# A four-layer perceiver on one core: late keys and values of layer four stored compactly, two units per context turn

## The reference, cut to what matters

```python
x = x + tanh(g_xattn[0]) * linear_attention(norm(x), ctx, mask)     # 16 heads
x = x + tanh(g_ffn[0])   * ternary_ffn(norm(x))
x = x + tanh(g_xattn[1]) * window_attention(norm(x), ctx)           # needs ctx rows 0..55 only
x = x + tanh(g_ffn[1])   * top2_of_16_experts(norm(x))
x = x + tanh(g_xattn[2]) * perceiver_attention(ctx, norm(x), mask)  # 8 heads, over ctx and latents
x = x + tanh(g_ffn[2])   * int8_ffn(norm(x))
x = x + tanh(g_xattn[3]) * attention(q=norm(x), k=ctx, v=ctx)       # 16 heads of 8
x = x + tanh(g_ffn[3])   * top2_of_8_experts(norm(x))
```

## Time and profile before

| | us |
|---|---|
| median of 3 runs | 881.52 (877.07 to 884.06) |
| the profiled execution | 890.45 |
| its span | 888.7 |
| PE, DVE, ACT, POOL busy | 758.9, 611.2, 415.3, 332.2 |

### The profile page before, as it was taken

The page is one execution under the profiler, slowest core; times in us unless marked ns, Lnnn a source line. Parts: engine busy times, 40 slices in busy tenths (PEclk is TensorE's granted clock), DMA queues, the critical chain, the costliest instruction groups (busy, mean ns, idle before and its releaser), DMA issues.

```text
span 888.7 us, 15989 instructions
## 1 busy us (share of the span) xinstructions
PE 758.9 (85%) x5636; PEld 500.2 (56%) x5636; DVE 611.2 (69%) x1270; ACT 415.3 (47%) x698; POOL 332.2 (37%) x269
## 2 busy tenths in 40 slices
PE   4699999974676678999699999998689999988996
PEld 4577777764444347664355555564336666554664
DVE  4789999994687425655656655557689999815652
ACT  2566666670454242452354454531027777654331
POOL 1765555550533440254087777750140000000111
PEclk9899999987888975999799999999959999999999
DMA  7366766423517533020504222207604565500220
GB/s 196 105 216 230 255 224 204 134 75 103 91 53 222 168 125 89 28 80 26 140 19 120 78 72 72 72 1 100 143 1 123 126 171 135 152 1 24 80 98 22
DMA packets 56610, 97.18 MB, mean 109 GB/s; under 512 B 16970, under 2 KB 41034, under 8 KB 55226
## 3 DMA queue, kind: packets, MB, share of 16 engines
q1 hardware_dynamic: 56546, 96.32, 38.0%
HBM read 64.65 MB, written 31.65 MB: 108 GB/s over the span
## 4 chain that ended last, share of the span: by engine, by line
PE 41%; DVE 32%; DMA 8%; ACT 6%; POOL 5%; issue 4%; SPq 3%; POOLq 0%; DVEq 0%; ACTq 0%
DVE arena L2324 8%; PE ps L1106 8%; DVE arena L1730 7%; PE ps L1096 6%; DMA d_v<-arena 5%; DVE rn L1885 4%; DVE arena L1934 3%; PE ps L1039 3%; PE ps L1274 2%; PE ps L1284 2%; PE ps L1209 2%; DVE arena L1913 2%; PE ps L1198 2%; DVE arena L1893 2%; ACT arena L1535 2%
## 5 line engine op out<-in xcount | busy, mean ns | idle before, releaser
L2324 DVE TENSOR_REDUCE arena<-ps 112x1 f32<-112x500 f32 x192 | 115.5, 669 | 15.1 <-PE ps L1183 14.2
L1730 DVE TENSOR_TENSOR arena<-ps,arena 128x448 f32<-128x448 f32 (+7 forms) x138 | 83.3, 628 | 60.5 <-ACT arena L1558 19.4
L1700 POOL TENSOR_TENSOR arena<-arena 125x448 f32<-125x448 f32 x96 | 109.6, 1142 | 24.1 <-ACT arena L1512 21.1
L1535 ACT ACTIVATE arena<-ps 125x896 f32<-125x896 f32 x96 | 87.0, 917 | 27.0 <-PE ps L1198 26.4
L1106 PE MATMUL ps<-arena 125*128 125x448 f32 (+1 forms) x208 | 97.0, 548 | 1.6 <-ACT arena L1512 1.2
L1592 POOL TENSOR_TENSOR arena<-arena 112x4 f32<-112x4 f32 x9 | 9.3, 1029 | 232.7 <-DVE arena L1754 226.7
L1512 ACT ACTIVATE arena<-arena,kbias 125x448 f32<-125x448 f32 x96 | 63.7, 668 | 65.3 <-DVE arena L1730 46.3
L1730 DVE TENSOR_TENSOR arena<-ps,rn 125x448 f32<-125x448 f32 x96 | 59.3, 618 | 47.7 <-PE ps L1096 43.3
L1096 PE MATMUL ps<-arena 128*125 128x448 f16 (+3 forms) x312 | 77.6, 359 | 3.0 <-DVEq L1741 3.0
L1096 PEld LDWEIGHTS ps<-arena 128*125 128x125 f16 (+1 forms) x312 | 40.8, 135 | 57.2 <-issue 42.3
L794 PE MATMUL ps<-w_k2h,arena 128*125 128x512 f16 x288 | 67.6, 387 | 6.1 <-ACT arena L1344 6.1
(11 more groups left out here) (308 smaller groups left out, 1477.3 us busy)
## 6 DMA issues: line engine op xcount, KB each, us to landing
d_k<-arena SPq DMA_DIRECT2D x24, 375.0 KB
d_v<-arena SPq DMA_DIRECT2D x24, 375.0 KB
arena<-d_k SPq DMA_DIRECT2D x96, 93.8 KB
arena<-d_v SPq DMA_DIRECT2D x8, 1008.0 KB
arena<-in_ctxT SPq DMA_DIRECT2D x8, 750.0 KB, 10.3
d_cln<-arena SPq DMA_DIRECT2D x8, 750.0 KB
d_clnT<-arena SPq DMA_DIRECT2D x8, 750.0 KB
arena<-d_clnT SPq DMA_DIRECT2D x8, 750.0 KB
```

Of the source, the lines that this page charges most:

```text
L1535: act.activation(p3[t % 2].rearrange("p (k h) q -> p k (h q)", k=2), ps[0:KP, 2 * (t % 2):2 * (t % 2) + 2, 0:8 * S], ACT.Exp).then_inc(l3_ ...
L1700: ins = pool.tensor_tensor(psum2[p][0:rows], psum2[p][0:rows], pexp[(t + p) % 2][0:rows], ALU.add)
L1730: return dve.tensor_tensor(out, a, b, op)
L2324: dve.tensor_reduce(mx3[bn % 2][:, u % 2, u % 8 // 2, u // 8:u // 8 + 1], ps[0:TT, max_bank_of(bn, u), 0:500], AX.X, ALU.max).then_inc(l3_ ...
```

## The change

- The f16 keys are stored as high and low alone (16 rows for 24 per four-head group), and the values as 128 columns instead of the padded 192. ACT copies the values in one piece; POOL's duplicate copy goes. Layer four loads the high part twice, and POOL spreads the values into the padded block (`spread_values3`) before PE uses it.
- Two units go with each turn (0 to 15), eight (16 to 23) with the chain, none inside layer two's attention; four buffers instead of three, and two f32 key buffers.
- The small loads of layer two go out after the turn of batch 6, and the 56 context rows per batch are loaded already turned (`c56T`), right after the pass; PE's transposes and ACT's copy of them go.
- In layer four, keys have three buffers in two parts; 8 maxima tiles instead of 4 run ahead of a batch (`MAX_AHEAD`), `turn_maxima` stands two steps before the last of a batch, the first scores of the next batch stand in the last step, and ACT writes both shift rows. DVE builds batch 0's query block from PSUM, ACT copies the queries for the others.
- At the last expert of both mixtures, DVE adds the earlier sum and the last term to `x` itself (`weigh_last`); POOL's loops over experts are written out.

```diff
-L1_LOADS = 5
+L1_LOADS = 4
+SETS = 4
...
-UNITS = [(b, 0) for b in range(B)] + [(b, third) for b in (7, 6, 0, 1, 2, 3, 4, 5) for third in (1, 2)]
-
-PRODUCT = {"latent_q": 14, "latent_k": 18, "latent_qT": 19, "queries2": 20}
...
+MAX_AHEAD = 32
 MAX_ORDER = [(0, u) for u in range(24)]
 for _b in range(1, B):
-    MAX_ORDER += [(_b, 0), (_b, 1), (_b - 1, TURN)] + [(_b, u) for u in range(2, 24)]
+    MAX_ORDER += [(_b, u) for u in range(4)] + [(_b - 1, TURN)] + [(_b, u) for u in range(4, 24)]
...
+            at = 500 * ((u - 18) % 3)
+            return wex[(u - 18) // 3][:, at:at + 500]
...
                 sp.wait_ge(d_free, 6 * b + 3 + 3)
                 sp.dma_start(batch(d_cln, b), cln[p].rearrange("p j d -> p (j d)")).then_inc(st[p], 16)
                 if more:
-                    sp.wait_ge(a_full, a_uses(b) + 8)
+                    sp.wait_ge(a_full, a_uses(b) + 10)
                     load_turned(b + 2, p)
                     sp.wait_ge(l0_rhs, b + 1)
                     load_context(b + 2, p)
+                if b == B - 1:
+                    store_later(2 * b)
+                    store_later(2 * b + 1)
+                    sp.wait_ge(ctx_done, 1)
+                    sp.dma_start(c56T, io["c56T"]).then_inc(l1_ld, 16)
                 sp.wait_ge(d_free, 6 * b + 3 + 6)
                 sp.dma_start(batch(d_clnT, b), clnT[p]).then_inc(st[p], 16)
-                store_later(b)
+                if b < B - 1:
+                    store_later(2 * b)
+                    store_later(2 * b + 1)
 
             def load_later(u):
                 b, third = UNITS[u]
...
+                if b == 6:
+                    for dst, name in ((w_l1, "L1_w"), (w_col1, "L1_cols"), (w_r1, "L1_router")):
+                        sp.dma_start(dst, io[name]).then_inc(l1_ld, 16)
...
-            store_later(8)
             sp.wait_ge(l0_att, 1)
...
-            for u in range(10, 13):
+            for u in range(16, 24):
                 store_later(u)
+                if u == 20:
+                    sp.wait_ge(lv_full, 20 - IN_TURNS + 1)
+                    load_experts1(0, 0)
+            sp.wait_ge(lv_full, 23 - IN_TURNS + 1)
+            load_experts1(1, 1)
             sp.wait_ge(rn_sq, 1)
-            for u in range(18, 24):
-                load_later(u)
-            for u in range(13, 24):
-                store_later(u)
-                if u == 14:
-                    sp.wait_ge(lv_full, 14 - B + 1)
-                    load_experts1(0, 0)
-                if u == 17:
-                    sp.wait_ge(lv_full, 17 - B + 1)
-                    load_experts1(1, 1)
-            sp.wait_ge(lv_full, 23 - B + 1)
             for dst, name in ((w_kT2, "L2_wkT"), (w_vT2, "L2_wvT"), (w_o2, "L2_wo"), (w_q2, "L2_wq"),
                               (qk_col, "qk_cols")):
                 sp.dma_start(dst, io[name]).then_inc(ld_m, 16)
@@ -628,8 +626,8 @@
 
             for p in range(2):
...
+                src = d_k3[b].rearrange("g e (d s) c -> e s d g c", s=2)
+                both = d_k3[b].rearrange("g e r c -> e r g c")
                 for hh in range(4):
-                    sp.dma_start(kst[p][32 * hh + 8:32 * hh + 32, :, at:at + 500], src[hh, :, :, at:at + 500])\
-                        .then_inc(l3_ld[p][u], 16)
+                    sp.dma_start(kst[p][32 * hh + 8:32 * hh + 24, :, cols], both[hh, :, :, cols]).then_inc(l3_ld[p][part], 16)
+                    sp.dma_start(kst[p][32 * hh + 24:32 * hh + 32, :, cols], src[hh, 0, :, :, cols])\
+                        .then_inc(l3_ld[p][part], 16)
...
+            for b in range(B - 2):
+                if b + 3 < B:
+                    sp.wait_ge(l3_s0, KT * b + 4)
+                    sp.wait_ge(l3_s, KT * b + 4)
+                    load_keys3(b + 3, b % 3, 0)
+                sp.wait_ge(l3_v, b + 1)
+                load_values3(b + 2, b % 2)
+                if b + 3 < B:
+                    sp.wait_ge(l3_s0, KT * (b + 1))
+                    sp.wait_ge(l3_s, KT * (b + 1))
+                    load_keys3(b + 3, b % 3, 1)
 
...
-                later_keys(cT[p][:, 0:4, :], bank_a(b, 6)).then_inc(a_full, 1)
-                later_values(cT[p][:, 0:4, :], bank_a(b, 7)).then_inc(a_full, 1)
+                for k in range(2):
+                    later_keys(cT[p][:, 4 * k:4 * k + 4, :], bank_a(b, 6 + 2 * k)).then_inc(a_full, 1)
+                    later_values(cT[p][:, 4 * k:4 * k + 4, :], bank_a(b, 7 + 2 * k)).then_inc(a_full, 1)
...
-            pe.wait_ge(l1_ld, L1_LOADS * 16)
-            for t in range(NT):
-                last = pe.transpose(ps[0:D, 0, TT * t:TT * t + TT], c56[:, t, :], ident[0:TT, 0:TT])
-            last.then_inc(l1_kv, 1)
...
+            pe.wait_ge(l1_ld, L1_LOADS * 16)
+            pe.matmul(ps[0:D, 1, 0:N], w_l1[:, 1, :], c56T, start=True, stop=True).then_inc(l1_kv, 1)
...
-                    later(13, 14, 15)
+                    later(20)
...
-            later(10, 11, 12)
+            later(18, 19)
...
-            later(16, 17, 18)
+            later(21, 22, 23)
...
-            later(19)
...
+                    elif b + 1 < B:
+                        sim3(b + 1, 0)
+                    for n in range(2):
+                        ahead = 2 * (KT * b + t) + MAX_AHEAD + n
+                        if ahead < 24 * B:
+                            max_sim(ahead // 24, ahead % 24)
+                    if t == KT - 3 and b + 1 < B:
+                        turn_maxima(b + 1)
...
-                h = u % 3
-                if u >= 3:
-                    act.wait_ge(st_l[h], 32 * (u // 3))
-                if u:
-                    act.wait_ge(l_lo, u if u < B else u - 1)
+                h = u % SETS
+                if u >= SETS:
+                    act.wait_ge(st_l[h], 32 * (u // SETS))
+                if u >= 2:
+                    act.wait_ge(l_lo, u - 1)
                 act.wait_ge(*keys)
                 act.copy(late_k3[h][:, 0, :], ps[0:D, k[0], 0:500])
-                act.copy(keys_rest(u), ps[0:D, k[0], 0:500]).then_inc(keys_taken(u)[0], 1)
+                act.copy(late_k[u % 2], ps[0:D, k[0], 0:500]).then_inc(keys_taken(u)[0], 1)
                 act.wait_ge(*values)
-                src = ps[0:KP, k[1], :].rearrange("p (j n) -> p j n", j=4)
-                act.copy(late_v[h][:, :, 0:128].rearrange("p j (g c) -> p j g c", c=32)[:, :, :, 0:24],
-                         src[:, :, 0:96].rearrange("p j (g c) -> p j g c", c=24))
-                act.copy(late_v[h][:, :, 128:192].rearrange("p j (g c) -> p j g c", c=16)[:, :, :, 0:HD16],
-                         src[:, :, 96:128].rearrange("p j (g c) -> p j g c", c=HD16)).then_inc(values_taken(u)[0], 1)
+                act.copy(late_v[h], ps[0:KP, k[1], :]).then_inc(values_taken(u)[0], 1)
 
             def later(*units):
                 for u in units:
...
+            act.wait_ge(product, PRODUCT["queries3T"])
+            act.wait_ge(l3_q, 1)
+            act.copy(q3, ps[0:D, 0:4, 0:N]).then_inc(l3_free, 1)
+
             def shift_rows3(b):
-
                 act.wait_ge(l3_sh, b + 1)
-                act.copy(qst3[64:68, b:b + 1, :, 2:4, :].rearrange("p o g h q -> p (o g) (h q)"),
-                         ps[64:68, max_bank_of(b, TURN), 0:TT].unsqueeze(1).broadcast_to([4, 4, TT]))\
-                    .then_inc(l3_row, 1)
+                for r, heads in ((0, slice(0, 2)), (64, slice(2, 4))):
+                    act.copy(qst3[r:r + 4, b:b + 1, :, heads, :].rearrange("p o g h q -> p (o g) (h q)"),
+                             ps[r:r + 4, max_bank_of(b, TURN), 0:TT].unsqueeze(1).broadcast_to([4, 4, TT]))\
+                        .then_inc(l3_row, 1)
+
+            def outputs3(b):
...
+                    if t == 0 and b:
+                        outputs3(b - 1)
+                    if t == KT - 3 and b + 1 < B:
+                        shift_rows3(b + 1)
+            outputs3(B - 1)
...
-                    k3 = late_k3[u % 3]
+                    k3 = late_k3[u % SETS]
                     pool.wait_ge(*keys_taken(u))
-                    pool.tensor_tensor(k3[:, 1, :], keys_rest(u), k3[:, 0, :], ALU.subtract).then_inc(l_lo, 1)
-                    pool.tensor_copy(k3[:, 2, :], k3[:, 0, :]).then_inc(l_dup, 1)
+                    pool.tensor_tensor(k3[:, 1, :], late_k[u % 2], k3[:, 0, :], ALU.subtract).then_inc(l_lo, 1)
 
...
+            def spread_values3(b):
+
+                p = b % 2
+                pool.wait_ge(l3_ldv[p], 32 * (b // 2 + 1))
+                if b > 1:
+                    pool.wait_ge(l3_pv, KT * (b - 1) + 2)
+                ch.step(pool.tensor_copy(v3s[p][:, :, 0:D].rearrange("p j (g c) -> p j g c", c=32)[:, :, :, 0:24],
+                                         v3c[p][:, :, 0:96].rearrange("p j (g c) -> p j g c", c=24)))
+                ch.link(pool.tensor_copy(v3s[p][:, :, D:].rearrange("p j (g c) -> p j g c", c=16)[:, :, :, 0:HD16],
+                                         v3c[p][:, :, 96:D].rearrange("p j (g c) -> p j g c", c=HD16)))
```

(19 more changed lines are left out.)

295 lines of the change are left out of this document (120 added, 175 removed).

## The result

The changed kernel took **876.19 us** (median of 20 runs, 869.89 to 881.82), the kernel before 887.92 on the same chips (20 runs); the ratio is **0.9886, 95% interval 0.9856 to 0.9916**. The forecast of 840 us and its range of 820 to 860 missed: the direction was right, and a quarter of the size came. Part of the miss is the base: the three runs shown first had a median of 881.52, the 20 of later 887.92, so the forecast as a ratio was 0.953, which on the later base is 846 us. The other 30 us are the prediction's own.

The account below looks back on a forecast made before the run. Bounds: nearly full PE and DVE in the context pass, waits from 203 to 358 us, DVE and batch joins in the fourth layer. 881.5 +10.3 -9.8 -2.8 -9.3 -18 -10.7 -1.3 gave 840 us, range 820 to 860.

Parts of the forecast that it names:

- Two units a turn: Context pass: more PE work and a bank wait, +1.4 us a turn for seven turns plus +0.5, sum +10.3.
- rival 3: Context pass: DVE's product of 1.75 us waits for POOL's remainder, 1.14 us in seven turns, +8, total 848; chance 0.05.
- The first turn: Context pass, first turn: one remainder more on its path, +0.5 us.
- rival 2: Context pass pays the whole bank wait, 24 us for 10, total 854; chance 0.12.
- Before the attention: Layer one: PE no longer stands 9.4 us for small loads, so its attention goes out earlier, -9.8 us.
- layer two's start: Earlier start carried on, less 0.5 us for the last three late units on PE: -9.3 us.
- layer two's attention: Without late units inside it, DVE is the longest and it takes 35 us for 53: -18, bounds -9 and -24.
- Store and load: Layer one's attention: store stays at 11.00 us (other end -3); its load no longer queues behind a unit's stores, -2.8 us.
- Fourth layer, start: DVE writes batch 0's queries straight from PSUM instead of POOL, so first scores start earlier: -3.1 us.
- Fourth layer, batches: Maxima end earlier, ACT writes both shift rows: 15.0 us per batch, between 14.4 and 16.1, six times -1.1.
- Half clock: Layer two's attention: PE at half clock adds about 4 us to its forecast length.

Follow-up runs that it names:

- Experiment 3: Changed kernel with POOL's two remainders of the late keys moved behind the affine steps in context turns: 870.10 us, 0.9786 of the kernel before.
- Experiment 1: Changed kernel with PE's sums of the turn before placed between the first and second unit of late keys and values: 865.47 us, 0.9738 of the kernel before.
- experiment 4: Changed kernel with sums ahead of the second unit, shift rows one exponential later, POOL's value-tile clears held back: 851.50 us, 0.9604 of the kernel before.
- Experiment 2: Changed kernel with ACT's two shift rows of the fourth layer copied one exponential later: 867.84 us, 0.9789 of the kernel before.
- five more moves: Changed kernel with sums ahead, shift rows later, POOL's clears held back, expert weights later, remainders behind affine steps: 847.33 us, 0.9560 of the kernel before.

## Why the prediction was wrong

- **Two units a turn** (+10.3, measured +19.2). The mechanism was named, and a steady turn cost +2.20 for +1.4: 0.80 for the work and a wait of 1.34 for 0.6. Experiment 3 splits that wait. With the remainders out of DVE's way it is 0.63, so the 0.6 was right. Its reason held too: PE's first key product starts 1.93 us before DVE's last statistics step there, for 2.93 before the change. The other 0.70 is rival 3.
- **Rival 3, the shared port** (0.05), is the step that failed in these turns. It was put at nothing in the sum because "PE being longer leaves DVE 0.8 us of slack". There was no slack to use: DVE stands 1.63 us for PE's sums inside the ring, and its product comes behind them, so every part of it lengthens the turn. It was not the product of 1.75 us that stood but the one in front of it, on 12 numbers, and 0.70 a turn, not 1.14: 3.5 us in five turns.
- **The first turn** (+0.5, measured +6.2) is the larger miss, 5.7 of the pass's 8.9. I counted one remainder on its path. It is a wait of 4.75 us at the same bank, because there the statistics wait for POOL, and half a clock behind it, which came in some executions only (31.5 to 32.9 us with it, 29.1 without). I had this bank in the steady turn and left it out of the first. The pass as a whole came near rival 2 (0.12), 19 us for its 24, by another way: that 24 took the wait of 1.7 in full and 1.7 of work, though its own rows leave 0.8 of work beyond the turn. Experiment 1 opens the ring and leaves +8.5.
- **Small DVE steps beside POOL elsewhere.** A wait of the same kind took 1.8 us at layer two's start and 2.1 in the second feed-forward, where the sum had 0; experiment 4 gives the latter back.
- **Before the attention and layer two's start** (-9.8, -9.3; measured -8.4, -7.8), **layer two's attention** (-18; -16.4): right in mechanism and near in size. ACT's 35.4 us of waits for value stores are gone, and DVE's 9.76 and 11.71 are 0.78 and 1.52.
- **Store and load** (-2.8, measured -6.1): the load gave 2.56 of the 2.8 forecast, the store 3.55 where the sum had 0 and the bound 3. Its pieces of 32 bytes are unchanged, so they alone did not set the 11.00. The cause is open.
- **Fourth layer, start** (-3.1, measured -3.2): right.
- **Fourth layer, batches** (six times -1.1, measured +1.0 in all). The term rested on the maxima being early. They are; the step that failed is the one on ACT. The prediction saw its two rows of 0.5 us and its slack of 0.26 a step, but left out that its queue is in order, so that the wait for the turned maxima (1.29) stands in front of a tile whose scores are ready. Experiment 2: 14.86 for 15.82. Against the kernel before, which alternated 15.76 and some 16.6, even the 15.82 won only 0.3 a batch, and the stop of PE beside the expert weights took 4.6 of it back. The transfers come 36 us earlier than before; that the three key buffers let SP run ahead is read from the program. I had looked at every queue but that one's end.
- **Half clock** was in the sum at one place, +4 in layer two's attention. In the first turn, at layer two's start, at the joins and behind the stop a pause of PE was paid twice in some executions: once as a wait and again at half clock. That the profiles lie 19.9 apart and the medians 11.7 fits this (mean clocks of 0.927 and 0.940 in the two profiles), but no run shows that it is all of it.
- The range should have reached 876. That the kernel with five more moves takes 847.33, 0.956 for the forecast 0.953, does not make the forecast right: those moves are not in the change.

## What to carry to other kernels

When work is added in front of a step that another engine waits for, draw the ring through the buffers, not only through the data: a bank freed by an engine that waits for statistics ties the added work to them, and an engine that waits inside the ring has no slack: whatever lengthens one of its steps behind that wait, by 0.70 us here, lengthens the turn. Put the step that is waited for ahead of the added work. A wait moved to an in-order engine must stand behind everything that is ready, and a clear or copy on POOL needs a place where DVE reads PSUM (two remainders took 2.10 us beside such a step, 3.69 beside DVE's products).

## What the runs showed of the hardware

- One DVE instruction on 112 x 4 numbers took 2.23 us for 0.17, and ended with POOL's clear beside it.
- PE stopped for 1.1 to 4.3 us behind its 4434th matmul in ten profiles, until 1.2 to 1.5 us after a 16 KB packet of the instruction queue had landed. Meanwhile weights came in in nine of them (at 390 GB/s in the changed kernel), keys and values in one (129 to 140); in three profiles where the packet came sooner PE stood 0.2 us or not at all.
- Without an edit near it, a stretch ran at a granted clock of 1.00 in one execution and 0.50 in another (14.5 or 18.0 us, batches of 15.8 or 17.2, a first turn of 29.1 or 32.7), each time behind pauses of PE; the same pauses also passed at 1.00.
